# A graph network in one TensorE-turned scan: the own rows' product one step earlier, and group 46's sums brought back ahead of turning group 47

## The reference

```
row, col = edges and one self-loop for each node
norm = deg_inv_sqrt[row] * deg_inv_sqrt[col]
h = x
for _ in range(16):
    h_neighbors = segment_sum(norm * h[row], col)
    h = 0.9 * h_neighbors + 0.1 * x
x = layernorm(x + h)
```

## Time and profile before

| | us |
|---|---|
| median of three runs | 8888.29 |
| lowest and highest run | 8879.96, 8893.03 |
| the profiled execution, own time | 8909.66 |
| its span, first to last instruction | 8907.8 |
| layer 2's passes in the trace | 4056 to 8106 |
| mean granted clock of TensorE | 0.663 |

### The profile page before, as it was taken

One profiled execution on the slowest core, in us unless ns is written; L12 is line 12 of the kernel. 1 busy time (PEld: TensorE's weight loads), 2 busy tenths in 40 slices (PEclk: granted clock), 3 DMA queues, 4 the chain that ended last, 5 costly groups with the idle time before them and its releaser, 6 DMA issues. The chain is left out here.

```text
span 8907.8 us, 120170 instructions
## 1 busy us (share of the span) xinstructions
PE 5427.0 (61%) x23642; PEld 4366.1 (49%) x23642; DVE 4880.4 (55%) x12177; ACT 1977.6 (22%) x5359; POOL 6617.4 (74%) x6942
## 2 busy tenths in 40 slices
PE   7666644444554444346777777777777667766643
PEld 6555633333333333214666666665555556655533
DVE  7687654555555556754555555554444444465543
ACT  2354631111111110633211111100000000065433
POOL 6677677777777777677777777777777777777777
PEclk9677855555655555556777887876766676665555
DMA  7664443343443333423444444433333333333311
GB/s 140 136 175 126 99 105 103 106 108 107 117 109 108 107 106 99 132 75 96 112 116 115 115 116 118 120 107 101 99 100 99 99 99 103 101 95 89 82 45 37
DMA packets 923001, 940.13 MB, mean 106 GB/s; under 512 B 398982, under 2 KB 814860, under 8 KB 922158
## 3 DMA queue, kind: packets, MB, share of 16 engines
q1 hardware_dynamic: 664502, 590.58, 22.1%
q0 software_dynamic: 221568, 316.85, 16.4%
q10 hardware_dynamic: 36186, 25.02, 1.0%
HBM read 560.22 MB, written 399.36 MB: 108 GB/s over the span
## 5 line engine op out<-in xcount | busy, mean ns | idle before, releaser
L1943 POOL DMA_INDIRECT l_g<-tab,l x2856 | 2704.2, 947 | 883.4 <-issue 802.4
L2150 DVE TENSOR_TENSOR_SCAN l_w<-l_m,l_w,bank 96x512 f32<-96x512 bf16 x1248 | 1591.9, 1276 | 2609.1 <-PE bank L1977 2592.3
L1977 PE MATMUL bank<-ident,l_g 128*96 128x128 f32 x4964 | 1139.7, 372 | 1609.2 <-DMA l_g<-tab,l 801.7
L1943 POOL DMA_INDIRECT l_g<-tab,XM x1716 | 1633.0, 952 | 530.4 <-issue 480.7
L1997 PEld LDWEIGHTS bank<-ident,l_w 96*128 96x128 f32 x6272 | 1601.6, 328 | 312.9 <-issue 236.0
L1977 PEld LDWEIGHTS bank<-ident,l_g 128*96 128x96 f32 x4964 | 765.0, 174 | 2018.5 <-DMA l_g<-tab,l 890.0
L1997 PE MATMUL bank<-ident,l_w 96*128 96x96 f32 x6272 | 1506.6, 401 | 7.7 <-DVE l_w L2150 7.2
L1988 PE MATMUL bank<-XM,ident 128*128 128x384 f32 x1568 | 902.1, 668 | 0.0
L310 PE MATMUL bank<-tail_xt,v 96*96 96x500 f32 (+1 forms) x298 | 277.0, 1030 | 380.5 <-ACT tail_xt L305 380.3
L2067 ACT ACTIVATE T<-T,dinv_e 128x96 f32<-128x96 f32 x196 | 57.0, 361 | 1941.1 <-DVE T L2175 1940.9
L421 ACT ACTIVATE tail_y<-bank,tail_of,tail_sc 125x96 f32<-125x96 f32 (+1 forms) x596 | 208.7, 430 | 1214.1 <-DVE tail_of L412 1047.3
(11 more groups left out here) (332 smaller groups left out, 9926.3 us busy)
## 6 DMA issues: line engine op xcount, KB each, us to landing
row_buffer<-tab ACTq DMA_DIRECT2D x9504, 0.4 KB
tab<-T SPq DMA_DIRECT2D x784, 192.0 KB
row_buffer<-tab SPq DMA_DIRECT2D x7392, 0.4 KB
tab<-l_o SPq DMA_DIRECT2D x441, 192.0 KB
l_m<-mask_d SPq DMA_DIRECT2D x784, 96.0 KB
l_m<-mask_s SPq DMA_DIRECT2D x490, 96.0 KB
l_g<-tab,l POOLq DMA_INDIRECT x2856
l_g<-tab,XM POOLq DMA_INDIRECT x1716
```

Source lines behind the costliest of these rows:

```text
L1943: nc.gpsimd.indirect_dma_start(out=tile(G[q % RG], t), out_offset=None, in_=tables[0:table_at + (2 - p % 2) * TR, :] if p else first, in_o ...
L1977: last = nc.tensor.transpose(a_bank(q)[0:D, u:GE:U], rows, self.ident[:, :])
L2150: v.tensor_tensor_scan(out=W[q % RW][:, :], data0=masks[q % RM][:, :], data1=a_bank(q)[0:D, :], initial=W[(q - 1) % RW][:, GE - 1:GE] if q ...
```

## The change

For the smooth mode only, `back_at(46)` becomes 47 and no longer 48, so that `backs(47)` is 45 and 46 and `backs(48)` is 47 alone. TensorE and VectorE both follow `backs`, and SP's stores too. And `add_own` leaves `turn_back`: the own product of the first group of `backs(g + 1)` is made in step g, after the background work and ahead of `turn(g)`; a second group of a step (46, in step 47) gets its own product directly ahead of being brought back. No instruction is added or left out.

```diff
         def back_at(g):
-            return g + 2 if g + 2 < NGP else g + 1
+            return g + 2 if g + 2 < NGP - smooth else g + 1
...
                 def turn_back(q):
-                    if smooth:
-                        add_own(q)
                     pe.wait_ge(scanned.sem, scanned.at + q + 1)
...
                 for p in range(K):
                     for g in range(steps_of):
                         for n in backs(g):
+                            if smooth and n != backs(g)[0]:
+                                add_own(p * NGP + n)
                             last = turn_back(p * NGP + n)
                         if looped and g < NGP:
                             background("pe", pe, p, g)
+                        if smooth and backs(g + 1):
+                            add_own(p * NGP + backs(g + 1)[0])
                         if conv and 0 <= g - 4 < NGP:
                             last = turn_sums(g - 4)
```

## The result

The changed kernel took 8935.38 us in the median of 6 runs (8931.52 to 8944.23), against 8886.7 us for the kernel before (6 runs, 8879.96 to 8893.03). The ratio is 1.0051, 95% interval 1.0041 to 1.0061: slower by about 45 us (the medians lie 48.7 us apart), outside the predicted range of 8877 to 8902. The profiled execution has a span of 8933.5 us.

The account below looks back on a forecast made before the run. GpSimd's gathers were taken as the bound, with 9.56 us of stalls between passes. Pass-end shifts of +2 us and -1 for the clock gave net +1 on the median of 8888.3: 8889 us, range 8877 to 8902.

Parts of the forecast that it names:

- Step 1 of the change part by part: Steps 1 to 46, own products one step earlier: same sum of work between turnings; taken as 0, bounds 0 to 1.28 us.
- The first paragraph: What bounds the kernel: GpSimd's gathers; TensorE matters only between passes, where 9.56 us of stalls are all to be won.
- Steps 2 to 4: Pass end, steps 47 to 49: the product of 48 ends 0.4 us later at low clock, 0.4 us earlier at high.
- the high-clock end of the sum: Pass end with TensorE's clock high: turn 48 at 6047.85 where it was 6048.27, 0.4 us earlier.
- the clock decides against it: Rival: exposed scan waits leave the lower clock at the first ten pass ends, 18 us more, 8906; chance 0.13.
- Steps 5 and 6: SP's last store still lands 2.75 us after its product, taken as 0; the last pass has 5 us of cover.
- the new order stalls inside a pass: Rival: turn g waits for VectorE where background work has TensorE late; 1.28 us in 16 passes, 20 us, 8909; chance 0.03.

Follow-up runs that it names:

- own_early_mid: The kernel before, with own products one step early up to step 40 only and pass ends as before; ratio 1.0020.
- own_early_from_pass_8: The changed kernel, but own products are early only in passes 8 to 15, which have no background work; ratio 0.9999.
- the twins: The kernel before with each own product made twice: the extra one a step early, ratio 1.0090, or in the old place, ratio 1.0023.
- own_early_at_end: The changed kernel, but own products are early only from step 41 on, where there is no background work; ratio 1.0019.
- back_only: The kernel before with only group 46 brought back in step 47, each own product staying directly ahead of bringing back; ratio 1.0003.
- own_ahead_of_background: The changed kernel, but the early own product stands ahead of the background work of its step, not behind it; ratio 1.0032.

## Why the prediction was wrong

**Step 1 of the change part by part failed**: "Its cover is TensorE's idle time before a landing ... I take 0; without that cover the order still has the same sum." The sum of TensorE's work between two turnings is the same, but not what lies in the waits. The cover was read from the earlier trace rows, the end of a pass, where no background work runs, and so was the step of 3.94 us that was held against the 5.0 us of a group. In steps 1 to 40 of passes 0 to 6 TensorE waits for ScalarE and VectorE inside the background work, twice in a cycle of six steps. The own product used to lie in front of that wait and now lies behind it. The two steps with such a wait took 6.8 and 7.7 us before and take 7.9 and 9.6 us now (medians); six steps went from 28.5 to 30.3 us, past the 29.1 us of the gathers, and the lag grows through the pass (16.6 us at most, 9.4 before). The term that was put at 0 measures 15.5 us of stalls and 0.20% by itself, in own_early_mid; own_early_from_pass_8 (nothing) and the twins (0.90% against 0.23%) show that it is the background work and the place.

**The first paragraph missed the row fetches.** That inside a pass "nothing on TensorE can slow it" held for the gathers, whose idle time put down to TensorE is 0.7 us at most. But GpSimd's restart waits for the whole chain, and SP's row fetches keep step with a late TensorE and stay late when it has caught up. Of the 48.4 us of stalls, 21.1 stay when only the steps from 41 on have the new order; of the other 27, 18 go when the rows are fetched one step earlier.

**Steps 2 to 4, the end of a pass**: their sum was right for an end at the low clock. In own_early_at_end turn 47 to turn 48 took 5.74 us (forecast 5.6), and the product of 48 ended 18.5 us after turn 46 in pass 0 (turn 46 at 4284.40, end at 4302.90; forecast 18.4). Four of the first ten ends were of this length (18.3 to 18.5 us), the other six 16.7 to 17.0. The size was off because the high-clock end of the sum never came: from turn 48 to the product of 48 all ten took 5.73 to 5.81 us, as long as the 5.74 of the earlier trace rows, where four of the ten took 5.27 to 5.39 before. So stalls were 21.1 us and not 10 to 12. That is part of the rival "the clock decides against it", which had 0.13; whether the empty waits brought the lower clock was not tested. What the prediction did not price is the move alone, with own 47 and own 48 left in the waits for the scans: back_only, whose stalls are half of those before. Taking them out of these waits is the second loss, with the clock that went with it; moving own 48 alone brings back 10 of the 16 us between back_only and own_early_at_end.

**Steps 5 and 6** hold: from the product of 48 to the restart are 2.76 us after pass 5 before and after the change, and GpSimd's pause behind the last lot of layer 2 is 5.22 us in both.

**The rival "the new order stalls inside a pass"** came nearest, with 0.03, and partly by luck. It named the right place, "where the background work already has TensorE late", but another mechanism: that the own product makes turn g wait for VectorE's bank. It never does; TensorE has no idle time before line 1988 in the changed kernel. Against it the prediction asked only for the seven gather buffers. Its 20 us were an own product for each of 16 passes; it is paid twice in each cycle of six steps, in seven passes.

## What to carry to other kernels

When a piece of work is moved in an in-order engine, ask in each kind of step which wait it lies in front of, and read a row of each kind; equal sums between two points say nothing if a wait for another engine stands between. Work moved from in front of a wait to behind it can cost its full length, and the price becomes a lag once the step is longer than the period of the engine that feeds it. A lag may be made up before it matters; so ask also which queues walk along with the late engine, and whether they catch up as fast. Here the row fetches on SP did not.

## What the runs showed of the hardware

Bringing back takes 1.84 us from its start to the next own product's when it follows a turning, and 1.71 to the next turning's when it follows an own product, both at the high clock (4982.36 to 4984.20 in own_ahead_of_background, 4994.13 to 4995.84 in the kernel before), so a step without a wait took 2.95 us in the new order and 2.80 in the old, for the same instructions. In passes without background work the new order ran at a mean granted clock of 0.57 from 6060 to 8060 us, where the old one had 0.69, and lost no time by it that own_early_from_pass_8 (0.9999) shows: there TensorE waits for landings either way.
